# Cross-attention kernel: turned probabilities moved by DMA to one partition per key, value products in one matmul per head

## The chip, the cores and the metric

One Trainium2 chip (trn2), one NeuronCore of it. The metric is the device time of one execution in microseconds (us); lower is better. A core has TensorE (matmuls into PSUM), VectorE (DVE), ScalarE (ACT), GpSimd (POOL) and SyncE (SP), which here only issues DMAs. Each engine runs its own instruction stream in order, and they are tied together by semaphores.

## What is computed

`x` is 2 x 2048 x 640, the context 2 x 77 x 1024, with 69 text tokens and 8 image tokens (4 dummy, 4 of boxes). There are 20 heads of 32 columns.

```python
q = split(x @ w_q)
k, v = split(text @ w_k), split(text @ w_v)
out_text = softmax(q @ k.T / sqrt(32)) @ v
k_ip, v_ip = split(ip @ w_k_ip), split(ip @ w_v_ip)
out_ip = softmax(q @ k_ip.T / sqrt(32) + mask(bbox)) @ v_ip
out = (merge(out_text) + merge(out_ip)) @ w_out + b_out + x
```

The mask is 0 or -10000 by the position of the query in a 32 x 64 grid. All is float32.

## The kernel before

The work is 40 units. Unit c (`place(c)`) is one batch (2), one tile of 512 queries (4) and one group g of 128 model columns, which is 4 heads (5 groups). For a unit there are:

- `make_q`: the q product, transposed (128 columns x 512 queries), 15 matmuls of 128x128x512 in fp32r. Each operand is split into a high and a low part, so each of the 5 contraction blocks takes three matmuls (`product`, L604). It goes to PSUM bank 4; ScalarE copies it to `q`.
- `make_scores` (L637): 32 small fp32 matmuls, queries in the rows, 77 keys in the columns, into banks 0 to 3, a head per bank, columns 0 to 307. An fp32 matmul is two instructions, each with its own weight load.
- VectorE subtracts the text maximum, adds the mask and subtracts the image maximum (L466 to L483); ScalarE takes the exponential (L372); VectorE sums (`sums`, L490 to L495); GpSimd multiplies by the reciprocals (L334, L336). The result is `prob`: 128 queries in the partitions, 16 (query block, head) pairs x 96 columns, of which 77 are keys and the rest zero.
- `turn` (L502): VectorE transposes each 32x32 block. Afterwards a partition 32a + i holds key 32kb + i for the queries of the block a, so keys of all three key blocks kb lie on the same 32 partitions and queries are spread over four groups of partitions.
- `make_o` (L656): because of that the value products are 48 matmuls of 32x32 weights and 128 moving columns: 3 key blocks (accumulated) x 4 partition groups a x 4 heads. They write to columns 320 to 447 of banks 0 to 3, beside the scores. V lies four times, once on each 32 partitions, in three key blocks (`vt`, `v_turn` L728: 6 transposes per group; `v` is 128 x 6 x 640).
- `o_high` (ScalarE, L407) and `o_low` (VectorE, L508) split the result for the output product.
- `make_out`: 15 matmuls like those of q, into bank 5, six units behind; `finish` (VectorE, L519) adds bias and residual; SyncE stores the tile.

The order is written out by hand for every engine in `step(c)`. TensorE in a middle step: scores of c+1, q of c+2, value products of c-1, output product of c-6. Since scores and value products share banks, the scores of c wait for `o_low` of c-3 and the value products of c-1 wait until the scores of c+1 have been used. VectorE in a middle step: shifts of c+1, `turn(c)`, `o_low(c-1)`, `sums(c+1)`, `finish(c-6)`. ScalarE: `copy_q(c+2)`, `o_high(c-1)`, `exp(c+1)`, the high parts of newly loaded tiles. Steps 0 to 5 also hold the making of K and V for each group (context products L684, image products L690, whose output goes to a column group of 32 for each contraction block, turns L728), and the last two steps and the epilogue hold the output products without q.

SyncE issues all DMAs in order: prologue loads, in each step the loads of the step (`step_jobs`), then the residual of c-5 (waits until the tile's last store has landed) and the store of c-6 (waits for `finish`). Its queue also holds the V loads of groups 2 to 4 in the prologue, two of which wait for slots.

Of the kernel before, what the change touches and what calls it, by code (L numbers as in the profile page):

```python
# [41 lines left out]
V_OLD = {3: 0, 4: 2}  # L42
X_JOBS = {0: (0, 1, 2), 1: (3, 4)}
# [4 lines left out]
def xattn_kernel(nc, x, ctx, bbox, grid, eye, w_q, w_k, w_v, w_k_ip, w_v_ip, w_out, b_out, out):  # L48
# [22 lines left out]
    with es:  # L71
# [14 lines left out]
        eye_sb = sb("eye_sb", [P, P + BATCH * (KEYS - TEXT)])  # L86
        ident = eye_sb[:, 0:P]
        fold = eye_sb[:, P:P + BATCH * (KEYS - TEXT)].rearrange("p (b n) -> p b n", b=BATCH)
        vt = sb("vt", [P, BATCH * KB, QB, SQ])
# [25 lines left out]
        Q_BANK, OUT_BANK, SPARE_BANK = 4, 5, 6  # L115
        LAST_BANKS = [Q_BANK, SPARE_BANK, OUT_BANK, 0, 1]
        O_COL = 320
        o_blocks = ps[:, 0:QB, O_COL:O_COL + QT * SQ].rearrange("p a (n r) -> p n a r", r=SQ)
# [5 lines left out]
        v_place = ps[:, V_BANK, 0:BATCH * KEYS].rearrange("p (b n) -> p b n", b=BATCH)  # L124
        v_turned = ps[:, V_BANK:V_BANK + 2, :].rearrange("p b (k n) -> p (b k) n", n=P)[:, 2:2 + BATCH * KB, :]
# [37 lines left out]
        turned = sem("turned")  # L163
        o_made = sem("o_made")
# [27 lines left out]
        def is_late(c):  # L192
            return c >= UNITS - LATE

# [24 lines left out]
        def _(sp):  # L219
# [33 lines left out]
            def prologue():  # L253
# [21 lines left out]
                for job in step_jobs(0):  # L275
                    load(job)
                load_v(1, wv_raw, w_v, wv_loaded)
                load_v(1, wvi_raw, w_v_ip, wvi_loaded)
                load_k(4, wk_raw, w_k, wk_loaded)
                load_k(4, wki_raw, w_k_ip, wki_loaded)  # L280
                for job in step_jobs(1):
                    load(job)
                sp.dma_start(bias[:, :], b_out).then_inc(bias_loaded, 16)
                for g in range(2, KD):
                    load_v(g, wv_raw, w_v, wv_loaded)
                    load_v(g, wvi_raw, w_v_ip, wvi_loaded)

            def step(c):
                if c >= 2:
                    for job in step_jobs(c):  # L290
                        load(job)
# [56 lines left out]
        def _(act):  # L348
# [40 lines left out]
            def copy_vt(g):  # L389

                act.wait_ge(vt_made, g + 1)
                if g > 0:
                    act.wait_ge(v_made, g)
                nc.scalar.activation(vt[:, :, :, :], v_place.rearrange("p b (k r) -> p (b k) r", r=SQ)
                                     .unsqueeze(2).to_broadcast([P, BATCH * KB, QB, SQ]), ACT.Copy).then_inc(vt_copied, 1)

            def copy_v(g):

                act.wait_ge(v_made, g + 1)
                nc.scalar.activation(v[:, :, P * g:P * g + P], v_turned, ACT.Copy).then_inc(v_copied, 1)  # L400

            def o_high(c):
                b, t, g = place(c)
                act.wait_ge(o_made, c + 1)
                if c >= 2 * KD:
                    act.wait_ge(out_made, (c // KD - 1) * KD)
                nc.scalar.activation(o_hi[:, b, g, :].rearrange("p (n a r) -> p n a r", a=QB, r=SQ), o_blocks,  # L407
                                     ACT.Copy).then_inc(o_hi_done, 1)
# [18 lines left out]
            def step(c):  # L427
                if c <= KD:
                    if c + AHEAD_K < KD:
                        copy_k(c + AHEAD_K)  # L430
                    if c > 0:
                        copy_v_part(c - 1)
                        copy_vt(c - 1)
                    exp(c + AHEAD_S)
                    if c > 0:
                        copy_v(c - 1)
                    copy_q(c + AHEAD_Q)
                    if c > 0:
                        o_high(c - 1)
                    if c + AHEAD_K + 1 < KD:  # L440
                        copy_k_part(c + AHEAD_K + 1)
                elif exists(c + AHEAD_Q):
                    copy_q(c + AHEAD_Q)
                    o_high(c - 1)
                    exp(c + AHEAD_S)
                else:
                    if exists(c + AHEAD_S):
                        exp(c + AHEAD_S)
                    o_high(c - 1)
# [8 lines left out]
        def _(dve):  # L458
# [38 lines left out]
            def turn(c):  # L497

                dve.wait_ge(prob_done, c + 1)
                if c >= 2:  # L500
                    dve.wait_ge(o_made, c - 1)
                nc.vector.transpose(prob_t[:, c % 2, :, :].rearrange("p n k -> p (n k)"),  # L502
                                    prob[:, c % 2, :, :].rearrange("p n k -> p (n k)")).then_inc(turned, 1)

            def o_low(c):
                b, t, g = place(c)
                dve.wait_ge(o_hi_done, c + 1)
                nc.vector.tensor_tensor(o_lo[:, b, g, :].rearrange("p (n a r) -> p n a r", a=QB, r=SQ), o_blocks,  # L508
                                        o_hi[:, b, g, :].bitcast(F32).rearrange("p (n a r) -> p n a r", a=QB, r=SQ),
                                        ALU.subtract).then_inc(o_lo_done, 1)  # L510

            def finish(c, bank=OUT_BANK):
# [4 lines left out]
                if c == 0:  # L517
                    dve.wait_ge(bias_loaded, 16)
                nc.vector.scalar_tensor_tensor(out=tile, in0=ps[:, bank, :],  # L519
# [49 lines left out]
            def step(c):  # L569
                late = c >= UNITS - AHEAD_Q  # L570
# [3 lines left out]
                if late:  # L574
                    finish(c - BEHIND_OUT)
                if c == UNITS - 1:
                    o_low(c - 1)
                turn(c)
                if (late or c <= KD) and exists(c + AHEAD_S):
                    sums(c + AHEAD_S)  # L580
                if exists(c - 1) and c < UNITS - 1:
                    o_low(c - 1)
                if exists(c + AHEAD_S) and not late and c > KD:
                    sums(c + AHEAD_S)
# [266 lines left out]
```

## Time and profile before

| what | us |
|---|---|
| median of 3 runs | 438.83 |
| lowest and highest | 437.2, 440.38 |
| the profiled execution's own time | 438.98 |
| span of its trace | 437.2 |
| TensorE busy | 420.8 |
| VectorE busy | 346.8 |
| GpSimd busy | 155.3 |
| ScalarE busy | 134.0 |

The profile is of one execution. The span is the time from the first to the last instruction that the profiler saw. Busy time of TensorE counts overlapping matmuls once; the start of one block of matmuls to the start of the next says more of what a block costs than the sum of its durations. L604 is line 604 of the kernel. A wait is put down to what ended it.

### The profile page before, as it was taken

Reading aid. Unit: us, or ns where it says so; the run is one execution under the profiler, and the core shown is the slowest. Engines: PE = TensorE matmul, PEld = TensorE weight load, DVE = VectorE, ACT = ScalarE, POOL = GpSimd, SP = SyncE. Lnnn points to the kernel's source line nnn. Section 1 sums busy time; section 2 is a strip of 40 time slices with the busy share of each in tenths; the row PEclk is TensorE's granted clock in tenths of the full one; section 3 lists DMA queues with packets and bytes.
Section 4 is the critical chain, followed back from the end, with each engine's and each line's share of the span. In section 5 each row is a group of like instructions: output and inputs, shape, how many; then the busy total and the mean of one; then the engine's idle time right before and its main releaser. Section 6 shows DMA issues by size and latency. Waiting matters only on the chain.

```text
span 437.2 us, 17242 instructions
## 1 busy us (share of the span) xinstructions
PE 420.8 (96%) x7970; PEld 326.7 (75%) x7970; DVE 346.8 (79%) x457; ACT 134.0 (31%) x196; POOL 155.3 (36%) x128
## 2 busy tenths in 40 slices
PE   4999799989999999999999999999999999999996
PEld 3788678767777777777777777777777777777785
DVE  4578477759888998899888988899888988888712
ACT  4255344434223322342223332332223422222200
POOL 0238222555343632255324622265225422322200
PEclk9999999989999999999999999999999999999999
DMA  8987224212214321331124211321134111122333
GB/s 293 385 298 270 90 79 156 75 55 81 81 50 147 99 74 51 124 99 49 59 82 157 74 51 49 123 99 73 51 118 127 51 51 49 57 69 60 110 124 121
DMA packets 22391, 47.14 MB, mean 108 GB/s; under 512 B 2864, under 2 KB 2992, under 8 KB 22320
## 3 DMA queue, kind: packets, MB, share of 16 engines
q1 hardware_dynamic: 22320, 46.05, 30.7%
q8 instruction: 62, 1.02, 1.0%
q14 instruction: 9, 0.07, 0.1%
HBM read 35.55 MB, written 10.49 MB: 105 GB/s over the span
## 4 chain that ended last, share of the span: by engine, by line
PE 95%; DVE 2%; issue 1%; DMA 1%; ACT 0%
PE ps L604 67%; PE ps L656 13%; PE ps L637 8%; PE ps L684 5%; PE ps L690 1%; DMA stage<-in_w_q 1%; PE ps L728 1%; DVE prob_t L502 0%; PE ps L708 0%; DVE text_max L466 0%; DVE prob L472 0%; DVE wq_lo L558 0%; DVE stage L519 0%; ACT wq_hi L362 0%; PE ps L723 0%
## 5 line engine op out<-in xcount | busy, mean ns | idle before, releaser
L334 POOL TENSOR_TENSOR prob<-prob,rden 128x1104 f32<-128x1104 f32 x40 | 82.4, 2060 | 238.3 <-DVE rden L495 238.3
L604 PE MATMUL ps<-x_hi,wq_hi 128*128 128x512 f32 x200 | 84.9, 425 | 6.2 <-DVE x_lo L562 6.2
L368 ACT ACTIVATE q<-ps 128x512 f32<-128x512 f32 x40 | 23.8, 596 | 202.2 <-PE ps L604 202.2
L604 PE MATMUL ps<-o_hi,wo_hi 128*128 128x512 f32 x200 | 82.7, 414 | 0.0
L604 PE MATMUL ps<-x_lo,wq_hi 128*128 128x512 f32 x200 | 79.8, 399 | 0.0
L604 PE MATMUL ps<-x_hi,wq_lo 128*128 128x512 f32 x200 | 79.6, 398 | 0.0
L604 PE MATMUL ps<-o_lo,wo_hi 128*128 128x512 f32 x200 | 79.1, 395 | 0.0
L604 PE MATMUL ps<-o_hi,wo_lo 128*128 128x512 f32 x200 | 79.0, 395 | 0.0
L502 DVE STREAM_TRANSPOSE prob_t<-prob 128x1536 f32<-128x1536 f32 x40 | 70.8, 1769 | 0.0
L490 DVE TENSOR_REDUCE den<-prob 128x16 f32<-128x1104 f32 x40 | 51.9, 1296 | 19.0 <-ACT prob L372 19.0
L466 DVE TENSOR_REDUCE text_max<-ps 128x16 f32<-128x1104 f32 x40 | 52.2, 1304 | 17.3 <-PE ps L637 13.2
L656 PE MATMUL ps<-prob_t,v 32*32 32x128 f32 x3840 | 59.4, 278 | 1.7 <-DVE prob_t L502 1.7
L656 PEld LDWEIGHTS ps<-prob_t,v 32*32 32x32 f32 x3840 | 44.9, 103 | 19.9 <-issue 12.7
L372 ACT ACTIVATE prob<-prob 128x1232 f32<-128x1232 f32 x40 | 49.7, 1244 | 12.4 <-DVE prob L483 12.4
L472 DVE TENSOR_TENSOR prob<-ps,text_max 128x1104 f32<-128x1104 f32 x40 | 52.0, 1299 | 0.0
L604 PEld LDWEIGHTS ps<-x_hi,wq_hi 128*128 128x128 f32 x200 | 38.3, 191 | 17.2 <-DVE wq_lo L558 6.2
L604 PEld LDWEIGHTS ps<-o_hi,wo_hi 128*128 128x128 f32 x200 | 37.4, 187 | 14.6 <-issue 7.0
L508 DVE TENSOR_TENSOR o_lo<-ps,o_hi 128x512 fp32r<-128x512 f32 x40 | 27.1, 677 | 24.0 <-ACT o_hi L407 24.0
L637 PEld LDWEIGHTS ps<-k,q 32*64 32x64 f32 x2560 | 32.0, 130 | 18.2 <-issue 17.5
L318 POOL TENSOR_TENSOR x_lo<-stage,x_hi 128x512 fp32r<-128x512 f32 x35 | 44.4, 1293 | 1.7 <-ACT x_hi L359 1.7
L604 PEld LDWEIGHTS ps<-x_hi,wq_lo 128*128 128x128 f32 x200 | 38.1, 191 | 8.8
L604 PEld LDWEIGHTS ps<-o_hi,wo_lo 128*128 128x128 f32 x200 | 37.5, 187 | 9.1
(55 smaller groups left out, 387.0 us busy)
## 6 DMA issues: line engine op xcount, KB each, us to landing
stage<-in_x SPq DMA_DIRECT2D x38, 256.0 KB, 3.3
res<-in_x SPq DMA_DIRECT2D x37, 256.0 KB, 2.7
out_tiles<-res SPq DMA_DIRECT2D x37, 256.0 KB, 2.1
wk_raw<-in_w_k SPq DMA_DIRECT2D x5, 512.0 KB, 7.0
wki_raw<-in_w_k_ip SPq DMA_DIRECT2D x5, 512.0 KB, 6.4
wv_raw<-in_w_v SPq DMA_DIRECT2D x5, 512.0 KB, 6.2
wvi_raw<-in_w_v_ip SPq DMA_DIRECT2D x5, 512.0 KB, 7.7
stage<-in_w_q SPq DMA_DIRECT2D x5, 320.0 KB, 6.7
```

Of the source, the lines that this page charges most:

```text
L318: nc.gpsimd.tensor_tensor(x_lo[:, b, kt, :], slot[:, 0:W], x_hi[:, b, kt, :].bitcast(F32), ALU.subtract).then_inc(stage_lo, 1)
L334: nc.gpsimd.tensor_tensor(e[:, :, 0:TEXT], e[:, :, 0:TEXT], rden[:, par, 0, :].unsqueeze(2).to_broadcast([P, QT * HG, TEXT]), ALU.mult)
L368: nc.scalar.activation(q[:, c % 2, :], ps[:, Q_BANK, :], ACT.Copy, scale=SCALE).then_inc(q_copied, 1)
L372: nc.scalar.activation(prob[:, c % 2, :, 0:TOKENS], prob[:, c % 2, :, 0:TOKENS], ACT.Exp).then_inc(exp_done, 1)
L466: nc.vector.tensor_reduce(text_max[:, par, :, :], s[:, :, :, 0:TEXT], AX_X, ALU.max).then_inc(text_max_done, 1)
L472: nc.vector.tensor_tensor(e[:, :, :, 0:TEXT], s[:, :, :, 0:TEXT], text_max[:, par, :, :].unsqueeze(3).to_broadcast([P, QT, HG, TEXT]), ALU ...
L490: nc.vector.tensor_reduce(den[:, par, 0, :], e[:, :, 0:TEXT], AX_X, ALU.add)
L502: nc.vector.transpose(prob_t[:, c % 2, :, :].rearrange("p n k -> p (n k)"), prob[:, c % 2, :, :].rearrange("p n k -> p (n k)")).then_inc(t ...
L508: nc.vector.tensor_tensor(o_lo[:, b, g, :].rearrange("p (n a r) -> p n a r", a=QB, r=SQ), o_blocks, o_hi[:, b, g, :].bitcast(F32).rearrang ...
L604: return nc.tensor.matmul(ps[:, bank, :], w[:, g, P * kt:P * kt + P], m[:, b, kt, :], start=(n == 0), stop=(n == 3 * KD - 1))
L637: last = nc.tensor.matmul(ps[at:at + P // 2, j, TOKENS * n:TOKENS * n + TOKENS], q[rows, c % 2, P * n + at:P * n + at + P // 2], k[rows, b ...
L656: last = nc.tensor.matmul(ps[DH * j:DH * j + DH, a, O_COL:O_COL + QT * SQ], v[rows, KB * b + kb, P * g + DH * j:P * g + DH * j + DH], p_t[ ...
```

## The change

Of each unit's turned probabilities 12 DMAs on SyncE's queue copy the blocks from `prob_t` to a new tile `prob_k`, in which key k lies on partition k, for all 512 queries. `turn` writes the key block outermost, so that a DMA's rows are 2 KB. The value products become one matmul per head: 77 partitions, 32 columns of weights, 512 moving columns, into bank 7 alone. They run two units behind instead of one, right behind the scores; q and output products follow. `o_high` and `o_low` go two units behind too and read one plain bank. V is kept once, 77 partitions for each batch, so it takes two transposes per group instead of six, and smaller copies. The waits between scores and value products for their shared banks go. SyncE's V loads move: groups 1 and 2 before the last K load in step 0, groups 3 and 4 in steps 1 and 3. In the tail the output product of unit 33 goes to the q bank, the last tile's products use banks 6, 0, 1, 2, 3, and the value products of the last unit stand among them.

```diff
-        v = sb("v", [P, BATCH * KB, D])
+        v = sb("v", [P, BATCH, D])
...
-        prob_t = sb("prob_t", [P, 2, QT * HG, KEYS])
+        prob_t = sb("prob_t", [P, 2, KB, QT * HG, SQ])
+        prob_k = sb("prob_k", [P, 2, QB, QT * HG, SQ])
...
-        vt = sb("vt", [P, BATCH * KB, QB, SQ])
+        vt = sb("vt", [P, BATCH, TOKENS])
...
-        Q_BANK, OUT_BANK, SPARE_BANK = 4, 5, 6
-        LAST_BANKS = [Q_BANK, SPARE_BANK, OUT_BANK, 0, 1]
+        Q_BANK, OUT_BANK, O_BANK = 4, 5, 7
+        LAST_BANKS = [6, 0, 1, 2, 3]
...
+        def moves(c):
+
+            return 16 * QB * KB * (c // 2 + 1)
...
+            def move(c):
+
+                sp.wait_ge(turned, c + 1)
+                if c >= 2:
+                    sp.wait_ge(o_made, c - 1)
+                for kb in range(KB):
+                    n = min(SQ, TOKENS - SQ * kb)
+                    for a in range(QB):
+                        sp.dma_start(prob_k[SQ * kb:SQ * kb + n, c % 2, a, :, :],
+                                     prob_t[SQ * a:SQ * a + n, c % 2, kb, :, :]).then_inc(moved[c % 2], 16)
...
+            def step(c):
+                for job in step_jobs(c):
                     load(job)
...
+                if c == 0:
+                    for g in range(1, 3):
+                        load_v(g, wv_raw, w_v, wv_loaded)
+                        load_v(g, wvi_raw, w_v_ip, wvi_loaded)
+                    load_k(4, wk_raw, w_k, wk_loaded)
+                    load_k(4, wki_raw, w_k_ip, wki_loaded)
+                if c in V_OLD_STEP:
+                    load_v(V_OLD_STEP[c], wv_raw, w_v, wv_loaded)
+                    load_v(V_OLD_STEP[c], wvi_raw, w_v_ip, wvi_loaded)
+                move(c)
                 if exists(c - BEHIND_OUT + 1):
                     residual(c - BEHIND_OUT + 1)
...
                 if c >= 2:
-                    dve.wait_ge(o_made, c - 1)
-                nc.vector.transpose(prob_t[:, c % 2, :, :].rearrange("p n k -> p (n k)"),
-                                    prob[:, c % 2, :, :].rearrange("p n k -> p (n k)")).then_inc(turned, 1)
+                    dve.wait_ge(moved[c % 2], moves(c - 2))
+                nc.vector.transpose(prob_t[:, c % 2, :, :, :].rearrange("p k n r -> p n k r"),
+                                    prob[:, c % 2, :, :].rearrange("p n (k r) -> p n k r", r=SQ)).then_inc(turned, 1)
...
                 if c < KD:
                     pe.wait_ge(k_copied, c + 1)
-                if c >= 3:
-                    pe.wait_ge(o_lo_done, c - 2)
...
-                pe.wait_ge(turned, c + 1)
+                pe.wait_ge(moved[c % 2], moves(c))
                 if c < KD:
                     pe.wait_ge(v_copied, c + 1)
-                if exists(c + 2):
-                    pe.wait_ge(scores_used, c + 3)
                 if c >= 1:
                     pe.wait_ge(o_lo_done, c)
-                for kb in range(KB):
-                    for a in range(QB):
...
+                p_k = prob_k[0:TOKENS, c % 2, :, :, :].rearrange("p a (n h) r -> p n a h r", h=HG)
+                for j in range(HG):
+                    last = nc.tensor.matmul(ps[DH * j:DH * j + DH, O_BANK, :],
+                                            v[0:TOKENS, b, P * g + DH * j:P * g + DH * j + DH], p_k[:, :, :, j, :],
+                                            start=True, stop=True)
...
                     make_scores(c + AHEAD_S)
+                    make_o(c - 2)
                     make_q(c + AHEAD_Q, whole)
-                    make_o(c - 1)
-                    if exists(c - BEHIND_OUT):
-                        make_out(c - BEHIND_OUT)
+                    make_out(c - BEHIND_OUT)
...
             def epilogue():
...
+                make_out(UNITS - BEHIND_OUT)
+                make_o(UNITS - 2)
+                pe.wait_ge(scores_used, UNITS)
+                for g in range(3):
+                    make_last(g, range(0, KD - 2))
+                make_o(UNITS - 1)
+                for g in range(3):
+                    make_last(g, range(KD - 2, KD - 1))
                 for g in range(3):
                     make_last(g, range(KD - 1, KD))
```

VectorE's step becomes shifts of c+1, `o_low(c-2)`, `turn(c)`, `sums(c+1)`, `finish(c-6)`; ScalarE's middle step `o_high(c-2)`, `exp(c+1)`, `copy_q(c+2)`.

## Rows read from the trace of the kernel before

**Rows 1.** Page, parts 1 and 4: busy time by engine; the chain by line.

```profile
PE 420.8 (96%) x7970; PEld 326.7 (75%) x7970; DVE 346.8 (79%) x457; ACT 134.0 (31%) x196; POOL 155.3 (36%) x128
...
PE ps L604 67%; PE ps L656 13%; PE ps L637 8%; PE ps L684 5%; PE ps L690 1%; DMA stage<-in_w_q 1%; PE ps L728 1%; DVE prob_t L502 0%; PE ps L708 0%; DVE text_max L466 0%; DVE prob L472 0%; DVE wq_lo L558 0%; DVE stage L519 0%; ACT wq_hi L362 0%; PE ps L723 0%
```

**Rows 2.** Chain by time (start us, us, what): middle step, last piece.

```profile
217.59 3.65 PE ps L604 x15
221.23 1.42 PE ps L656 x79
222.65 3.70 PE ps L604 x15
226.34 0.88 PE ps L637 x57
...
416.22 17.70 PE ps L604 x75
```

**Rows 3.** VectorE's timeline, a middle step (start us, us, what, idle before).

```profile
227.26 1.31 DVE L466 TENSOR_REDUCE text_max<-ps 128x16 f32<-128x1104 f32 x1
...
230.55 1.77 DVE L502 STREAM_TRANSPOSE prob_t<-prob 128x1536 f32<-128x1536 f32 x1
232.95 0.69 DVE L508 TENSOR_TENSOR o_lo<-ps,o_hi 128x512 fp32r<-128x512 f32 x1 [0.63 <-ACT o_hi L407]
234.09 1.30 DVE L490 TENSOR_REDUCE den<-prob 128x16 f32<-128x1104 f32 x1 [0.45 <-ACT prob L372]
...
236.90 1.31 DVE L466 TENSOR_REDUCE text_max<-ps 128x16 f32<-128x1104 f32 x1
```

**Rows 4.** SyncE's queue: what it waited for (us in total, times, longest us).

```profile
SPq L251 <- DVE res L519: 237.7, 37, 9.0
```

**Rows 5.** Chain by time, early: image products, context products, turns of V.

```profile
19.62 0.57 PE ps L690 x16
...
22.47 1.88 PE ps L684 x16
...
38.65 0.66 PE ps L728 x6
```

**Rows 6.** Groups by line and form (xcount | busy us, mean ns | idle before).

```profile
L656 PE MATMUL ps<-prob_t,v 32*32 32x128 f32 x3840 | 59.4, 278 | 1.7 <-DVE prob_t L502 1.7
...
L690 PE MATMUL ps<-wki_raw,ctx_sb 128*32 128x128 f32 x80 | 3.2, 279 | 0.0
```

**Rows 7.** Waits of all engines (us in total, times, longest us).

```profile
PE ps L656 <- DVE prob_t L502: 1.7, 3, 1.0
```

**Rows 8.** Chain by time: the stall in step 2, step 5's end.

```profile
45.48 2.20 issue
...
85.36 1.47 PE ps L656 x75
...
87.76 0.61 ACT q L368
...
89.67 0.94 PE ps L637 x50
90.61 5.23 PE ps L604 x15
```

**Rows 9.** Windows: busy us by engine, then granted clock, DMA share, GB/s.

```profile
92.00:94.00 2.00, 2.00 (x6) 1.58 (x5) 1.93 (x5) 0.00 (x0) 1.19 (x1) 0.50 0.53 181
```

**Rows 10.** SyncE's timeline: DMA issues, at the start and in a middle step.

```profile
4.48 0.67 SPq L259 DMA_DIRECT2D grid_sb<-in_grid  x1
...
227.55 1.40 SPq L227 DMA_DIRECT2D stage<-in_x  x3
229.23 0.33 SPq L247 DMA_DIRECT2D res<-in_x  x1
```

**Rows 11.** Page, parts 3 and 6: packets, MB, share; us to landing.

```profile
q1 hardware_dynamic: 22320, 46.05, 30.7%
...
out_tiles<-res SPq DMA_DIRECT2D x37, 256.0 KB, 2.1
```

More of the change, by code:

```diff
@@ L42 @@
 V_OLD = {3: 0, 4: 2}
+V_OLD_STEP = {V_OLD[g] + 1: g for g in V_OLD}
 X_JOBS = {0: (0, 1, 2), 1: (3, 4)}
@@ L163, in xattn_kernel @@
         turned = sem("turned")
+        moved = [sem(f"moved{k}") for k in range(2)]
         o_made = sem("o_made")
@@ L274, in prologue @@
                 load_k(3, wki_raw, w_k_ip, wki_loaded)
-                for job in step_jobs(0):
+                sp.dma_start(bias[:, :], b_out).then_inc(bias_loaded, 16)
+            def step(c):
+                for job in step_jobs(c):
                     load(job)
[L277 to L291, printed above, removed]
+                if c == 0:
[8 more added lines that the diff above has]
+                move(c)
                 if exists(c - BEHIND_OUT + 1):
@@ L573, in step @@
                     shift_img(c + AHEAD_S)
-                if late:
+                if exists(c - 2):
+                    o_low(c - 2)
+                if c == UNITS - 1:
                     finish(c - BEHIND_OUT)
-                if c == UNITS - 1:
-                    o_low(c - 1)
                 turn(c)
-                if (late or c <= KD) and exists(c + AHEAD_S):
+                if exists(c + AHEAD_S):
                     sums(c + AHEAD_S)
[L581 to L584, printed above, removed]
-                if exists(c - BEHIND_OUT) and not late:
+                if exists(c - BEHIND_OUT) and c < UNITS - 1:
                     finish(c - BEHIND_OUT)
@@ L589, in epilogue @@
                 finish(UNITS - BEHIND_OUT)
-                o_low(UNITS - 1)
+                for c in range(UNITS - 2, UNITS):
+                    o_low(c)
                 for c in range(UNITS - KD, UNITS):
@@ L666, in make_out @@
                     pe.wait_ge(stage_lo, NUMBER[("w_out", g)] + 1)
-                if c >= 1:
-                    pe.wait_ge(finished, c)
+                if out_bank(c) == Q_BANK:
+                    pe.wait_ge(q_copied, UNITS)
+                elif c >= 1:
+                    pe.wait_ge(finished, c if out_bank(c - 1) == OUT_BANK else c - 1)
                 for n in whole:
-                    last = product(OUT_BANK, wo_hi, wo_lo, o_hi, o_lo, b, g, n)
+                    last = product(out_bank(c), wo_hi, wo_lo, o_hi, o_lo, b, g, n)
                 last.then_inc(out_made, 1)
@@ L722, in v_fold @@
                 pe.wait_ge(v_part_copied, g + 1)
-                nc.tensor.matmul(v_place[:, :, TEXT:KEYS], img_part[:, 1, :], fold, start=True, stop=True).then_inc(vt_made, 1)
+                nc.tensor.matmul(v_place[:, :, TEXT:TOKENS], img_part[:, 1, :], fold, start=True, stop=True).then_inc(vt_made, 1)
             def v_turn(g):
                 pe.wait_ge(vt_copied, g + 1)
-                for n in range(BATCH * KB):
-                    last = nc.tensor.transpose(v_turned[:, n, :], vt[:, n, :, :].rearrange("p a r -> p (a r)"), ident)
+                for b in range(BATCH):
+                    last = nc.tensor.transpose(v_turned[:, b, :], vt[:, b, :], ident)
                 last.then_inc(v_made, 1)
@@ L760, in early_step @@
                     v_turn(c - 1)
[L761 to L767 removed]
+                    make_q(c + AHEAD_Q, whole[9:15])
                 if c < 2:
```

75 lines of the change are left out of this document (27 added, 48 removed).

## The prediction

> **What bounds the kernel now.** I read the page first, then the chain of waits in order of time, then each engine's timeline over one middle step, SyncE's waits last. TensorE is busy for 420.8 us of 437.2, and the chain that ends last is TensorE almost all through: 67% products (L604), 13% value products (L656), 8% scores (L637) [rows 1]. In the chain a middle step is four blocks without idle time between them: q product 3.65, value products 1.42, output product 3.70, scores 0.88, in all 9.65 us [rows 2]. So a microsecond taken off TensorE in a middle step comes off the span, until another engine needs the whole step. VectorE is the nearest: from one text_max to the next 9.64 us, of which it idles 0.63 and 0.45 [rows 3], so its work is 8.56 us. That is the floor of a step as long as VectorE's work stays what it is. SyncE does nothing for most of the time: it waits 237.7 us in all for the finished tile [rows 4].
>
> **The change part by part.** All sums are made against the profiled execution: 438.98 us, 1.8 of it outside the span of 437.2. The median of the runs shown is 438.83, so the forecast for one is that for the other.
>
> *Value products.* Removed: 3840/40 = 96 TensorE instructions per unit on 32x32 tiles, 1.42 us from the block's start to the next. Added: 4 fp32 matmuls per unit (one per head, 77 partitions in, 32 columns of weights, 512 columns moving), each of two instructions, as all fp32 matmuls are here (48 matmuls give 96 instructions now). The trace has no such matmul, but it has its parts. An fp32 instruction that moves 138 columns takes 1.88/16 = 0.118 us, one of 128 columns 0.66/6 = 0.11 us, so 0.85 ns a column [rows 5]. Whether four heads run side by side is the main question. The image products (L690) are of the same form: all rows, 32 columns of weights, the four column groups in turn, another moving operand for each. 16 instructions of 128 columns take 0.57 us [rows 5, 6]; one after the other they would take 16 x 0.11 = 1.7. So four run together: 4 waves of 0.11 and some 0.13 for start and end. With 512 columns: 2 waves of 4 x 0.11 = 0.87, and 0.13, so 1.00 us. Bounds: 0.87 (no overhead) to 8 x 0.43 = 3.5 us (heads one after the other). I take 1.00, since L690 is the same shape but for its length. Gain: 0.42 x 40 = 16.8 us. The Trainium skill is a little more careful: "TensorE: Matmul & The Clock Gate", Part 3 (Packing small matmuls), gives 2.38 times the speed, not 3, for three column tiles of 32 with 512 columns; for four heads in the same proportion I estimate 3.2 times, so 4 x 0.87/3.2 = 1.1 us and a sum of 413. In the trace L690 comes to 1.7/0.57 = 3.0 times with its start and end in it.
>
> *Order on TensorE.* The value products move behind the scores, so q and output products stand next to each other. A block of 15 takes 3.70 and one of 75 takes 17.70 [rows 2]: 14.0/60 = 0.233 each, and 0.20 per block for changing over. One change-over less per step: 0.20 x 32 steps (6 to 37) = 6.4 us. Bounds 0, if what stands at a block's start is the wait and not the change of form, and 0.27 a step (3.65 + 3.70 - 30 x 17.70/75).
>
> *V plain.* Of 6 turns of V per early step, 2 remain: 4 x 0.11 x 5 = 2.2 us less [rows 5]. ScalarE's copies of it get smaller, which lies beside TensorE.
>
> *Early waits.* Now make_o(c-1) waits in the step in which its turn is made: 1.7 us on that tile's turn [rows 7], which in step 5 holds the products back until 85.36 [rows 8]. With a step more in between this goes. At the end of step 5 the scores wait for o_low in their own banks: TensorE ends the product at 87.76, where the copy of q begins, and starts again at 89.67, 1.91 us on [rows 8]. Value products have their own bank now, so only the copy of q (0.61, some 0.7 with its start) is left: gain 1.2. Behind this gap the clock is granted at 0.50 (1.2 GHz) for 92 to 94 [rows 9], and the q product takes 5.23 instead of 3.65: 1.6 us that I count as gained, since there is hardly a gap before it. The stall of 2.20 us inside the scores at 45.48 is put down to "issue" [rows 8]; nothing in the diff addresses it, but fewer instructions and another order of loads stand there; I count 1.1 of 0 to 2.2. New order of the early loads (V groups 1 and 2 before the last K): all have over 10 us until they are read; but I set 0.5 against it for a wait not foreseen.
>
> *The moves.* 12 DMAs per unit, 77 x 4 = 308 rows of 2 KB, 480 DMAs in all, on SyncE's queue between the loads and residual and store. Issue: 1.40/3 = 0.47 us each in a series, 0.67 for the worst kind in the trace [rows 10]; 0.33 is what a single one takes. I take 0.47, as all large ones in a series take this: 5.6 us per unit. Landing 2.1 as for the stores [rows 11]. In a step: scores end at 0.9, turn runs 4.8 to 6.6, moves are issued until 12.2 and have landed by about 14.3 from the step's start. They are needed two steps on, at 2 x 9.0 + 0.9 = 18.9, which leaves 4.6 us. SyncE per step: 5.6 + 2 x 0.33 for residual and store + at most 1.4 for loads = 7.7 of 9.0 us. Queued behind the wait for the turn are residual and store: the residual lands around 15, its finish comes at 18; the store is issued some 3 us later than now and its tile is needed again later still. Transfer: 22320 packets take 30.7% of 16 engines, 96 ns each [rows 11]; 308 x 96/16 = 1.9 us per unit, 17% of the engines' time over the span, beside 31% now. So all of it is hidden. In the tail it is less so: turn(38) ends 6.6 us into step 38, moves land at 14.3, TensorE is ready for O(38) at about 13.8: 0.5 us lost. O(39) stands behind 27 products (6.4 us), which cover its moves by about 1 us.
>
> *VectorE.* The turn writes the same 48 blocks to another place, 1.77 us as now [rows 3] (bounds 1.7 to twice that); o_low reads one bank plainly, 0.69 or a little less. The work stays 8.56 us.
>
> *Sum.* A middle step becomes 9.65 - 0.42 - 0.20 = 9.03 us, above VectorE's 8.56. In all 16.8 + 6.4 + 2.2 + 1.7 + 1.2 + 1.6 + 1.1 - 0.5 - 0.5 = 30.0, so 438.98 - 30.0 = 409.0 us.
>
> **The rivals.**
> *SyncE's queue becomes the bound; slower.* The step would be 12 issues and about 1.3 us for the rest. Above 0.64 us an issue this exceeds 9.03; from about 0.71 on the step is longer than now, as the value products then wait for the moves in each step. For it: 12 small DMAs a unit, a third of them of 13 partitions, a shape that the trace lacks, and 0.67 us for the smallest loads. Against: these lie in a full queue at the start and consist of short rows; the moves have 2 KB rows. At 0.80 us: 9.6 + 1.3 = 10.9 a step, 1.25 more than now in 34 steps, less 9 us of early gains: about 472 us. The Trainium skill, "DMA: Bandwidth & Descriptors", Rules for kernel authors, speaks for this rival: it tells to coalesce many small transfers, since below 64 KB one pays mostly overhead; the moves are of 64 and 26 KB. The trace agrees only in that a small load takes no less time to issue than a large one.
> *VectorE becomes the bound.* If the turn is slower with its split destination by over 0.47 us, the step is VectorE's. At twice its time: 8.56 + 1.77 = 10.33 a step, 0.7 more than now: 438.98 + 34 x 0.7 - 9 = 454. For it: 89% of the step is VectorE's already. Against: same number of blocks and bytes.
> *Heads one after the other.* 3.5 us a unit instead of 1.0: 409 + 100 = 509. Only the length differs from L690, so this is unlikely.
> *Half the side gains fail.* The step's order gives nothing, the clock falls in another place, the stall at 45 stays: 16.8 + 2.2 remain, 438.98 - 19 = 420. For it: TensorE gaps early moved before, and loads share the DMAs with moves there.
>
> **How the numbers follow.** Forecast (403 to 415) 0.68, side gains fail (415 to 425) 0.18, SyncE 0.06, VectorE 0.05, one after the other 0.03. The range from 402 to 425 holds the first two and leaves out the rest. A measurement here tells about 1% from no change: faster by over 1% 0.86, within 1% 0.04 (where SyncE or VectorE take back just the gain), slower 0.10.
>
> **What would show it.** Right: the value products are 320 instructions in blocks of about 1.0 us behind the scores; 30 products in one piece of about 7.15 us; middle steps of 9.0 us; no idle TensorE before the value products in steps 3 to 37; moves of 0.47 us, the last landing 4 us or more before its use; the turn at 1.77 us. Wrong: value products waiting for DMA prob_k in each step (SyncE), scores waiting for VectorE (VectorE), blocks of 3.5 us (no concurrency), 0.9 to 1.6 us more somewhere in the first 90 us (side gains).

## The result and the profile after

| | before | changed |
|---|---|---|
| median | 439.61 us (4 runs) | 483.72 us (4 runs) |
| lowest to highest | 437.2 to 441.04 | 478.04 to 485.29 |
| ratio, 95% interval | | 1.0943 (1.0885 to 1.1001) |

The changed kernel is slower by 9.4%, where 409.0 (402 to 425) was forecast. The profiled execution took 485.29 us, with a span of 483.5. The medians hold all executions, while each ratio leaves out those that stood apart from the rest of their kernel, here the one of 485.29 us, the profiled one, 0.3% above the median.

From the page of the changed kernel (span, part 1, the clock of part 2, part 3, both lines of part 4, three groups of part 5):

```profile
span 483.5 us, 10674 instructions
...
PE 419.3 (87%) x4430; PEld 303.4 (63%) x4430; DVE 335.5 (69%) x457; ACT 130.6 (27%) x196; POOL 155.9 (32%) x128
...
PEclk9999898898997999999899999899998999898959
...
q1 hardware_dynamic: 41840, 71.29, 51.2%
...
SPq 74%; PE 9%; issue 6%; DMA 5%; DVE 4%; ACT 1%; DVEq 0%
SPq L256 64%; PE ps L617 6%; SPq L267 3%; SPq L236 3%; SPq L271 3%; PE ps L692 1%; DMA stage<-in_x 1%; DVE prob_t L518 1%; DMA res<-in_x 1%; DMA prob_k<-prob_t 1%; DMA x_raw<-in_x 1%; PE ps L662 1%; DVE text_max L482 1%; DVE prob L488 1%; PE ps L698 0%
...
L536 DVE SCALAR_TENSOR_TENSOR res<-ps,bias,res 128x512 f32<-128x512 f32 x37 | 27.7, 751 | 93.6 <-DMA res<-in_x 79.3
...
L662 PE MATMUL ps<-prob_k,v 77*32 77x512 f32 x320 | 45.2, 638 | 30.9 <-DMA prob_k<-prob_t 21.4
L518 DVE STREAM_TRANSPOSE prob_t<-prob 128x1536 f32<-128x1536 f32 x40 | 70.7, 1767 | 0.0
```

The chain has changed hands. Before, it was TensorE for all but 5% [rows 1 give its lines: 67, 13 and 8%]; now 74% of it is SyncE's queue, and 64% of the span is one line of it, L256, the issue of the moves. TensorE is busy for about as long as before (419.3 for 420.8 us) in spite of 3540 fewer matmul instructions; the granted clock, which the page shows below 9 tenths in many slices, is 0.94 in the mean, 0.995 before. The run with four moves, further down, has the same 4430 instructions, a clock of 1.0 in the mean, and is busy for 392.7 us. VectorE waits before finish (L536) for 93.6 us, of which the residual's DMA ends 79.3. The turn takes 1767 ns, as before [rows 3], and it holds nothing up. The DMA engines' share is 51.2%, 30.7% before [rows 11].

A middle step in SyncE's queue, from the chain of the changed kernel in order of time (start us, us, what):

```profile
227.74 0.52 SPq L267
...
228.31 0.42 SPq L271
...
228.83 0.57 SPq L256
...
230.72 0.59 SPq L256
...
231.35 1.80 SPq L256
...
233.20 0.59 SPq L256
...
235.10 0.82 SPq L256
...
237.60 0.74 SPq L256
238.38 0.52 SPq L267
...
238.96 0.42 SPq L271
...
239.80 0.57 SPq L256
```

There is no gap: residual (L267), store (L271), twelve moves (L256), residual, store, and the moves of the next unit. From residual to residual it is 238.38 - 227.74 = 10.64 us; the queue never waits for anything in it. A move of 32 partitions takes 0.59 us and 0.04 to the next, one of 13 partitions 0.82, 0.78, 0.75, 0.74. One move of these takes 1.80. Before, a large issue took 0.47 in a series [rows 10], and SyncE spent 237.7 us waiting for finished tiles [rows 4]. What is left of its waits now (us in total, times, longest; L241 is a load of K at the start):

```profile
SPq L241 <- PE ps L716: 14.2, 2, 7.3
SPq L256 <- DVE prob_t L518: 8.8, 3, 4.5
...
SPq L267 <- DMA out_tiles<-res: 5.7, 2, 2.9
SPq L271 <- DVE res L536: 2.6, 2, 2.2
```

Who waits for SyncE instead, from all engines' waits:

```profile
DVE res L536 <- DMA res<-in_x: 79.3, 30, 11.6
...
PE ps L662 <- DMA prob_k<-prob_t: 21.4, 21, 3.6
...
PE ps L662 <- DVE o_lo L524: 9.4, 1, 9.4
```

Where the time went by part: the scores of unit 7 begin at 89.39 and those of unit 39 at 429.29 (TensorE's timeline).

```profile
89.39 0.82 PE L648 MATMUL ps<-k,q 32*64 32x77 f32 x52 [0.69 <-ACT q L386]
...
429.29 0.92 PE L648 MATMUL ps<-k,q 32*64 32x77 f32 x62
```

So the 32 middle steps take (429.29 - 89.39)/32 = 10.62 us each, 9.65 before [rows 2], 9.03 in the forecast. Single ones are not alike: ten of them are of 9.00 to 9.03 us, and those in which TensorE waits have up to 16.9 us. From there to the end of the span it is 54.2 us.

### The profile page after: what moved, and what is told of

It is laid out like the page before. It is cut to its first block, busy times and chain, and to the rows that moved or that the text cites. A ratio compares the mean times of both kernels' runs of the same rounds, so it can differ in the third digit from the quotient of the medians.

```text
span 483.5 us, 10674 instructions
## 1 busy us (share of the span) xinstructions
PE 419.3 (87%) x4430; PEld 303.4 (63%) x4430; DVE 335.5 (69%) x457; ACT 130.6 (27%) x196; POOL 155.9 (32%) x128
## 2 busy tenths in 40 slices
DMA packets 41888, 71.97 MB, mean 149 GB/s; under 512 B 10064, under 2 KB 10192, under 8 KB 41840
## 3 DMA queue, kind: packets, MB, share of 16 engines
q1 hardware_dynamic: 41840, 71.29, 51.2%
## 4 chain that ended last, share of the span: by engine, by line
SPq 74%; PE 9%; issue 6%; DMA 5%; DVE 4%; ACT 1%; DVEq 0%
SPq L256 64%; PE ps L617 6%; SPq L267 3%; SPq L236 3%; SPq L271 3%; PE ps L692 1%; DMA stage<-in_x 1%; DVE prob_t L518 1%; DMA res<-in_x 1%; DMA prob_k<-prob_t 1%; DMA x_raw<-in_x 1%; PE ps L662 1%; DVE text_max L482 1%; DVE prob L488 1%; PE ps L698 0%
## 5 line engine op out<-in xcount | busy, mean ns | idle before, releaser
L617 PE MATMUL ps<-o_hi,wo_hi 128*128 128x512 f32 x200 | 85.5, 428 | 18.2 <-DVE o_lo L524 17.7
L536 DVE SCALAR_TENSOR_TENSOR res<-ps,bias,res 128x512 f32<-128x512 f32 x37 | 27.7, 751 | 93.6 <-DMA res<-in_x 79.3
L617 PE MATMUL ps<-o_lo,wo_hi 128*128 128x512 f32 x200 | 83.4, 417 | 0.0
L617 PE MATMUL ps<-o_hi,wo_lo 128*128 128x512 f32 x200 | 82.9, 415 | 0.0
L662 PE MATMUL ps<-prob_k,v 77*32 77x512 f32 x320 | 45.2, 638 | 30.9 <-DMA prob_k<-prob_t 21.4
L518 DVE STREAM_TRANSPOSE prob_t<-prob 128x1536 f32<-128x1536 f32 x40 | 70.7, 1767 | 0.0
L617 PEld LDWEIGHTS ps<-o_hi,wo_hi 128*128 128x128 f32 x200 | 40.5, 203 | 35.2 <-DVE o_lo L524 20.5
L506 DVE TENSOR_REDUCE den<-prob 128x16 f32<-128x1104 f32 x40 | 50.6, 1265 | 9.1 <-ACT prob L390 9.0
L424 ACT ACTIVATE o_hi<-ps 128x512 fp32r<-128x512 f32 x40 | 23.6, 591 | 105.3 <-PE ps L662 105.3
L617 PEld LDWEIGHTS ps<-o_hi,wo_lo 128*128 128x128 f32 x200 | 40.3, 201 | 10.2
L617 PEld LDWEIGHTS ps<-o_lo,wo_hi 128*128 128x128 f32 x200 | 40.6, 203 | 9.3
L377 ACT ACTIVATE x_hi<-stage 128x512 fp32r<-128x512 f32 x35 | 21.8, 630 | 82.3 <-DMA stage<-in_x 82.0
```

Of the source, the lines that this page charges most:

```text
L424: nc.scalar.activation(o_hi[:, b, g, :], ps[:, O_BANK, :], ACT.Copy).then_inc(o_hi_done, 1)
L506: nc.vector.tensor_reduce(den[:, par, 0, :], e[:, :, 0:TEXT], AX_X, ALU.add)
L518: nc.vector.transpose(prob_t[:, c % 2, :, :, :].rearrange("p k n r -> p n k r"), prob[:, c % 2, :, :].rearrange("p n (k r) -> p n k r", r= ...
L617: return nc.tensor.matmul(ps[:, bank, :], w[:, g, P * kt:P * kt + P], m[:, b, kt, :], start=(n == 0), stop=(n == 3 * KD - 1))
L662: last = nc.tensor.matmul(ps[DH * j:DH * j + DH, O_BANK, :], v[0:TOKENS, b, P * g + DH * j:P * g + DH * j + DH], p_k[:, :, :, j, :], start ...
```

## The experiments

Theory A: SyncE's queue is the bound by its number of issues, at 0.63 to 0.86 us each. Theory B: the moves' transfer or landing is the bound. Theory C: the order is, since the residual now stands behind the moves. All ratios are to the kernel before in the same session (medians 440.17, 441.0 and 440.46 us). Differences from the changed kernel's 483.72 us are taken across sessions, between which the kernel before moved by 0.3% (439.61 to 441.0 us).

**Third key block as 16 partitions.**

```diff
-                    n = min(SQ, TOKENS - SQ * kb)
+                    n = min(SQ, TOKENS + 3 - SQ * kb)
```

> The third key block is moved as 16 partitions (keys 64 to 79, three of them zero columns) instead of 13; all else stays. Theory A (SyncE's issue of the moves is the bound; a 13-partition move takes 0.75 to 0.82 us to issue, a 32-partition one 0.59, because of its odd number of partitions): each of the 4 falls to about 0.59, 0.75 us less per unit, 27 to 30 us less in all, about 454 us. Theory B (the transfer or the landing of the moves is the bound): 3/77 more rows, so 483 or a little more. Theory C (the residual stands behind the moves and comes too late for finish): as A in proportion to the issue, a fall of at most 0.7 us a step.

Measured: 457.96 us, ratio 1.0403 (1.0335 to 1.0472). 26 us less than the changed kernel (483.72), though each of the 160 moves of the third block carries three rows more. The group of all 480 moves (duration ns min/median/max):

```profile
L256 SPq DMA_DIRECT2D prob_k<-prob_t x480: 507/590/2161, 32.6 to 434.9; - x160
```

The four issues of 0.74 to 0.82 us in the chain above are 0.59 us here, as A has it; the fall of 26 us is just short of the 27 to 30 expected. B is out for this part: more rows were moved, not fewer. C expected a fall of this size too, so the run says nothing against C.

**Four of the twelve issued by ScalarE.**

```diff
-                for kb in range(KB):
+                for kb in range(KB - 1):
...
+            def move_last(c):
+                act.wait_ge(turned, c + 1)
+                if c >= 2:
+                    act.wait_ge(o_made, c - 1)
+                kb = KB - 1
+                n = TOKENS - SQ * kb
+                for a in range(QB):
+                    act.dma_start(prob_k[SQ * kb:SQ * kb + n, c % 2, a, :, :],
+                                  prob_t[SQ * a:SQ * a + n, c % 2, kb, :, :]).then_inc(moved[c % 2], 16)
```

> The four 13-partition moves of each unit are issued by ScalarE, behind its copy of q; the eight others stay on SyncE. The same bytes are moved. Theory A: SyncE needs 8 x 0.63 + 1.05 for residual and store + about 0.6 for loads = 6.7 us a step, below TensorE's 9.0, so it is no longer the bound: 408 to 425 us. Theory B: the DMA engines move the same rows, so 475 to 490. Theory C: the residual comes 3.2 us earlier, so most of the gain too.

Measured: 424.64 us, ratio 0.9638 (0.9611 to 0.9665). The same rows and bytes, through the same 16 DMA engines, in as many DMAs that have to land, and 59 us less than the changed kernel: what bound it was SyncE's queue, not the transfer or the landing. C, by which the earlier residual gives most of the gain, is not out yet. Its waits, first in SyncE's queue, then all engines' (here ScalarE's):

```profile
SPq L256 <- DVE prob_t L530: 58.2, 37, 6.1
```

```profile
ACT x_hi L377 <- issue: 45.6, 12, 4.6
```

SyncE has time again (58.2 us waiting for the turn). ScalarE pays: 45.6 us in which its copies of x stand behind its own issues, and some products wait for that.

**Four moves a unit instead of twelve.** Only the first key block is moved.

```diff
-                for kb in range(KB):
+                for kb in range(1):
...
-            return 16 * QB * KB * (c // 2 + 1)
+            return 16 * QB * (c // 2 + 1)
```

> Left out: only the first key block is moved (4 DMAs a unit instead of 12); the other partitions of the moved tile are set to zero once. Theory A: SyncE is idle for most of the step and the rest of the forecast is laid open: middle steps of 9.0 us and 405 to 415 us in all. Theory B expects the same here. If the other terms of the forecast (value products 1.0 us, one change-over less, early waits) are wrong as well, it stays above 420.

Measured: 407.68 us, ratio 0.9256 (0.9232 to 0.9279). This is the forecast without the term that was wrong. A and B expect the same here, so the run does not tell them apart; it shows the other terms. A step in the chain of this run (start us, us, what):

```profile
206.09 0.99 PE ps L663 x8
207.08 7.13 PE ps L618 x30
214.21 0.88 PE ps L649 x56
215.09 0.99 PE ps L663 x8
```

Value products 0.99 (forecast 1.00, 1.42 before [rows 2]), q and output products in one piece of 30 in 7.13 (7.35 in two pieces before), scores 0.88: 9.00 us a step, where 9.03 was worked out. SyncE waits for the turn, longest in this list:

```profile
SPq L256 <- DVE prob_t L519: 165.1, 40, 6.1
```

The scores of units 7 and 39 begin here at

```profile
78.12 0.95 PE L649 MATMUL ps<-k,q 32*64 32x77 f32 x64 [0.69 <-ACT q L387]
...
367.42 0.80 PE L649 MATMUL ps<-k,q 32*64 32x77 f32 x50
```

which is 9.04 us a step. Against this run the changed kernel loses 89.39 - 78.12 = 11.3 us up to unit 7, 339.9 - 289.3 = 50.6 in the middle and 54.2 - 38.0 = 16.2 from unit 39 on: 78.1, the whole difference of the spans (483.5 - 405.4).

**The residual ahead of the moves.**

```diff
-                move(c)
                 if exists(c - BEHIND_OUT + 1):
                     residual(c - BEHIND_OUT + 1)
+                move(c)
```

> The residual is issued ahead of the moves in each step; the number of issues is the same. Theory A (rate of the queue): within 1.5% of the changed kernel, 476 to 490 us, and finish no longer waits for the residual, but the value products wait for the moves instead. Theory C (order): the wait of finish for the residual, 79 us in all, goes and with it most of the loss: below 455 us.

Measured: 511.55 us, ratio 1.1533 (1.1445 to 1.162). Neither theory expected 28 us more than the changed kernel. Its chain in order of time and, below it, SyncE's waits say why:

```profile
237.53 2.19 DMA out_tiles<-res
...
239.74 0.34 SPq L267
```

```profile
SPq L267 <- DMA out_tiles<-res: 48.7, 35, 2.4
```

From all engines' waits of this run:

```profile
PE ps L662 <- DMA prob_k<-prob_t: 57.9, 32, 4.3
...
DVE res L536 <- DMA res<-in_x: 5.8, 1, 5.8
```

The residual needs the tile whose store has just been issued. Behind the moves that store has long landed; ahead of them SyncE stands idle for its landing, 48.7 us in all in 35 waits or 1.4 us each. From unit 7 to unit 39 the first moves of two units are 11.50 us apart in the mean, in the changed kernel 10.67: (11.50 - 10.67) x 32 = 26.6 us, nearly the difference of the spans (510.5 - 483.5 = 27.0). Of the 48.7 us 5.7 were there before. Of the 43.0 that are new, 11 are got back in shorter issues (all of SyncE's sum to 400 us instead of 411), and its other waits change by less than 2 us each; the few us that are left were not traced. C is refuted: its own wait is gone (finish waits 5.8 us for the residual instead of 79.3), and the loss is not. What grew is the wait of the value products for the moves, 57.9 for 21.4, as A has it. A's size failed all the same, since it did not foresee the new wait: this queue has next to no time to spare, so most of a new wait in it comes out at the end.

**Half the bytes.** Each move takes half of each row.

```diff
-                        sp.dma_start(prob_k[SQ * kb:SQ * kb + n, c % 2, a, :, :],
-                                     prob_t[SQ * a:SQ * a + n, c % 2, kb, :, :]).then_inc(moved[c % 2], 16)
+                        sp.dma_start(prob_k[SQ * kb:SQ * kb + n, c % 2, a, 0:8, :],
+                                     prob_t[SQ * a:SQ * a + n, c % 2, kb, 0:8, :]).then_inc(moved[c % 2], 16)
```

> Left out: each of the 12 moves takes only the first half of each row (1 KB of 2 KB); the other half of the moved tile is set to zero once. Number of issues and of rows stay, the bytes are halved. Theory A (cost per issue): 0.59 and 0.78 us an issue as before, within 1.5% of the changed kernel, 476 to 490 us. Theory B (bytes, transfer): the issues get shorter and 20 us or more are won, below 465.

Measured: 475.65 us, ratio 1.0799 (1.0765 to 1.0834). This is 1.7% below the changed kernel's median, just outside what A expected; B's 20 us are not there. Twelve issues in this run (SyncE's timeline), 8.25 us, which is 8 x 0.63 and 4 x 0.80:

```profile
232.72 8.25 SPq L256 DMA_DIRECT2D prob_k<-prob_t  x12
```

The time of an issue does not hang on its bytes: for each of the twelve places in a unit the median over all units is that of the changed kernel to 0.001 us. The moves sum to 328 us for 336, and the difference lies in moves of over 0.9 us, 22 here and 27 there; why there are fewer was not tested.

**By way of DRAM, 4 DMAs a unit.** One DMA writes the turned tile out, three read it back with the keys in order.

```diff
+                sp.dma_start(via[c % 2], prob_t[:, c % 2, :, :, :].rearrange("p k n r -> p k (n r)")).then_inc(written[c % 2], 16)
...
+                for kb in range(KB):
+                    n = min(SQ, TOKENS + 3 - SQ * kb)
+                    sp.dma_start(prob_k[SQ * kb:SQ * kb + n, c % 2, :, :, :].rearrange("p a n r -> p a (n r)"),
+                                 via[c % 2].rearrange("(a i) k x -> i a k x", i=SQ)[0:n, :, kb, :]).then_inc(moved[c % 2], 16)
```

> The same result with 4 DMAs a unit instead of 12, all on SyncE: one writes the turned tile (128 partitions, 6 KB rows) to DRAM, and behind the store three read it back, one per key block (32, 32 and 16 partitions, 4 rows of 2 KB each). Theory A: at 0.45 to 0.60 us an issue 2.1 us of moves a step, SyncE is off the bound, and the time is that of the run with 4 moves, 407 to 414 us, as long as both trips (2.5 to 3.5 us each) fit into the 12 us between turn and use. Theory B: twice the DMA traffic of the changed kernel's moves, so no better than 475. If the round trip is too long for the tail: 3 to 6 us above 410.

Measured: 424.35 us, ratio 0.9636 (0.9597 to 0.9676), above the 407 to 414 of A. SyncE's timeline of a step, and below it all engines' waits (here TensorE's):

```profile
220.03 1.30 SPq L263 DMA_DIRECT2D prob_k<-via  x3
...
225.16 0.33 SPq L254 DMA_DIRECT2D via<-prob_t  x1
```

```profile
PE ps L670 <- DMA prob_k<-via: 12.2, 5, 5.5
```

The issues are cheap, 1.30 us for three and 0.33 for one, and 30 of the 32 middle steps take 8.99 to 9.02 us. What is lost is lost in a few places: 12.2 us of waiting in 5 times, the longest 5.5 us in step 2 (behind the scores of unit 3), where the first unit's write and reads stand behind the big loads of K and V. The theory's size for the landing, 2.5 to 3.5 us, was too low: in the middle the write lands after 3.9 us in the median and the reads after 4.2 and 4.6, and early the write takes 7.5. In the middle the two trips still fit between turn and use.

**ScalarE with 16 partitions.**

```diff
-                n = TOKENS - SQ * kb
+                n = TOKENS + 3 - SQ * kb
```

> As the run with ScalarE issuing the third key block, but with 16 partitions instead of 13. ScalarE's four issues take 0.6 instead of 0.8 us, 2.4 instead of 3.3 us a step, and its copies of x behind them and of the next value products come 0.8 us earlier. Theory: if ScalarE's blocked time is what holds the run with 13 at 424.6 above 407.7, half to all of it goes: 409 to 417 us. If it is the DMA traffic, it stays at 423 to 427.

Measured: 422.85 us, ratio 0.9584 (0.9535 to 0.9633): 1.8 us less than with 13 partitions, at the edge of what the runs tell apart. The edit took little of ScalarE's blocked time away (its copies of x stand 35.7 us behind its own issues instead of 45.6), so this run alone does not clear it. The last run below does: there it is 40.6 us, at a time of 412.08. The trace puts a loss elsewhere: 6.5 us in one piece before the value products of unit 39. It is there in the changed kernel too, where it is 9.45 us:

```profile
452.75 8.26 SPq L256 DMA_DIRECT2D prob_k<-prob_t  x12
461.06 0.52 SPq L267 DMA_DIRECT2D res<-in_x  x1
...
464.34 0.75 DVE L536 SCALAR_TENSOR_TENSOR res<-ps,bias,res 128x512 f32<-128x512 f32 x1 [11.62 <-DMA res<-in_x]
465.01 0.68 DVE L524 TENSOR_TENSOR o_lo<-ps,o_hi 128x512 fp32r<-128x512 f32 x1
...
465.83 1.94 PE L662 MATMUL ps<-prob_k,v 77*32 77x512 f32 x8 [9.45 <-DVE o_lo L524]
```

(Changed kernel, the timelines of SyncE, VectorE and TensorE.) The twelve moves of unit 39 stand ahead of the residual of unit 34; finish(34) waits for that residual, `o_low(38)` stands behind it on VectorE, and the last value products need `o_low(38)`. TensorE starts them at 465.83, 9.45 us late. The forecast priced the moves of the tail, but not what is queued behind them.

**Both repairs.** Units 0 to 4, 38 and 39 move directly, with 4 (at the end 6) of 12 issues on ScalarE; units 5 to 37 go through DRAM; the loads of V groups 1 and 2 stand behind the first moves; in the last two steps the residual stands ahead.

```diff
+        def direct(c):
+            return c < KD or c >= UNITS - 2
...
+                if c >= UNITS - 2:
+                    residual(c - BEHIND_OUT + 1)
+                if direct(c):
+                    move_part(sp, c, split(c)[0])
+                else:
+                    write(c)
+                if c == 0:
+                    for g in range(1, 3):
+                        load_v(g, wv_raw, w_v, wv_loaded)
+                        load_v(g, wvi_raw, w_v_ip, wvi_loaded)
```

> A kernel that is to keep the gains, with the reference's output. Units 0 to 4 and 38, 39: direct moves (third key block as 16 partitions), part of them issued by ScalarE (4 of 12, at the end 6 of 12); units 5 to 37: the way through DRAM, 4 DMAs. In step 0 the loads of V groups 1 and 2 stand behind the moves, in the last two steps the residual stands ahead of them. Theory (what is left above the run with 4 moves is early moves behind big loads and the late residual at the end): middle steps 9.0, step 3 under 12, step 39 to the end about 39, so 408 to 414 us. If DMA traffic in the early part is at fault: 416 to 422.

Measured: 413.0 us, ratio 0.9401 (0.9351 to 0.945), as expected. The middle steps are of 9.06 us, step 3 of 10.8 (under 12 expected), and from the scores of unit 39 to the end it is 40.6 us, where about 39 was expected.

**Three DMAs of 128 partitions.** A measurement of the issue itself; keys are not rearranged.

```diff
+                for kb in range(KB):
+                    sp.dma_start(prob_k[:, c % 2, kb, :, :], prob_t[:, c % 2, kb, :, :]).then_inc(moved[c % 2], 16)
```

> Left out: the rearranging. Each unit moves its turned tile by 3 DMAs of 128 partitions (64 KB becomes 256 KB each), partition to same partition, so keys are not in order. It measures what one DMA from SBUF to SBUF costs in issue. If 0.59 us is the price of both ends in SBUF: 0.59 here too. If it is the price of few partitions: 0.43 to 0.47, as the loads of 128 partitions. Either way 1.3 to 1.8 us a unit, and the time is that of the run with 4 moves, 405 to 412, though more bytes are moved than in the changed kernel (786 KB for 631).

Measured: 405.79 us, ratio 0.9231 (0.9168 to 0.9293). SyncE's timeline, three issues together:

```profile
221.09 1.76 SPq L254 DMA_DIRECT2D prob_k<-prob_t  x3
```

The first takes 0.47 us, the two others 0.60 and 0.62. So 0.6 us is the price in a series of a DMA with both ends in SBUF, of 32 partitions or of 128; the loads from DRAM that follow one another take 0.43 to 0.47 in the same queue. The residual, also a load from DRAM, takes 0.60 here, where it stands directly behind the third move, and 0.33 to 0.34 where the queue was idle before it (the kernel before [rows 10] and the run with the residual ahead). So the price may in part be that of standing behind a move; the runs do not tell the two apart. And 786 KB a unit in three DMAs cost nothing that can be seen, where 631 KB in twelve cost 78 us: the bytes are out. With the run of four issues on ScalarE, in which all twelve still have to land, B is out altogether.

**Direct moves, split over two queues, with the repairs.** As the kernel with both repairs, with no unit by way of DRAM: 8 issues on SyncE and 4 on ScalarE a unit, 6 and 6 for the last two.

```diff
-            return c < KD or c >= UNITS - 2
+            return c < UNITS or c >= UNITS - 2
```

> As the kernel before in this list (early order, residual ahead at the end), but all units move directly, 8 issues by SyncE and 4 by ScalarE, 6 and 6 for the last two units. Theory: the same early part and end; the middle steps cost what they do in the run with 16 partitions on ScalarE (9.0 to 9.2), so 2 to 5 us more than the kernel by way of DRAM: 411 to 418.

Measured: 412.08 us, ratio 0.9374 (0.9308 to 0.944). One of the four executions took 634.95 us at a mean granted clock of 0.563, where the three others took 408.87 to 412.71 at 0.995 or more; no cause was found for it. From the page of the one of 408.87 us (span, busy time, granted clock in 40 slices):

```profile
span 407.1 us, 10712 instructions
...
PE 394.5 (97%) x4430; PEld 289.2 (71%) x4430; DVE 335.1 (82%) x457; ACT 129.7 (32%) x196; POOL 155.6 (38%) x128
...
PEclk9999999999999999999999999999999999999999
```

It beats the kernel before by 6.3% (the kernel by way of DRAM has 6.0%; the intervals overlap, so which is better stays open) and the changed one by 14%. In the profiled execution the clock stays at 9 tenths or more in all 40 slices. What the two repairs give can be read by part: against the run with 16 partitions on ScalarE, from which it differs in them alone but for two issues in each of the last two units, the span is 4.9 us shorter up to the scores of unit 7, 1.5 in the 32 steps behind them, and 8.6 from unit 39 on.

## Why the prediction was wrong, point by point

**The step that failed** is the price of a move: "I take 0.47, as all large ones in a series take this: 5.6 us per unit." It measured 0.63 us from start to start for 32 partitions and 0.78 to 0.86 for 13, 8 x 0.63 + 4 x 0.81 = 8.3 us a unit, and in most units one issue is longer still (1.80 in the step shown), so the twelve take up to 9.9 us, 8.9 in the mean of the middle steps (0.74 each); from the first move of unit 7 to that of unit 39 a unit takes 10.67 us in the mean. The bound of 0.67 from the small loads stood in the text, and even without the long issues the mean of 0.69 (8.3/12) lies just above it. The sum took its price from loads out of DRAM that follow one another; the moves go from SBUF to SBUF, and the trace of the kernel before had no row of that kind.

**SyncE per step**, 7.7 of 9.0 us: it was 10.6 in the step shown. With it fell "So all of it is hidden".

**The rival that came true** is SyncE's queue, which had 0.06. The measured price is on its side of its point of decision (0.64 us an issue for being the bound), and its 472 us at 0.80 was nearer than the forecast. Its price for the rest of the queue, 1.3 us, was too low: residual, store, loads and short waits take 1.8 us in the mean of the middle steps. That shows in the run with 16 partitions: at 0.68 us an issue this rival's sum gives a step of 9.5 us, shorter than the 9.65 of before, and the step measured is 10.0. It left out that the tail loses in proportion: 16.2 us from unit 39 on, where I had 0.5 us.

**Heads side by side**: right. 0.99 us for 1.00. In the trace the first instructions of the four heads start within 0.02 us of each other, and the second ones 0.45 us later. One after the other the eight would take 3.4 us by the prediction's price, so four heads side by side are 3.5 times as fast. The estimate from the proportion in the Trainium skill ("TensorE: Matmul & The Clock Gate", Part 3) was 1.1 us, somewhat more than measured.

**One change-over less**: right. 7.35 became 7.13, 0.22 for 0.20.

**Early waits, clock and stall**: right in kind, as the run with four moves shows, and too low in size. It loses 0.69 us at the end of step 5 (0.7 forecast), the scores of unit 3 have no stall, and all 40 slices of its page have a granted clock of 9 tenths or more. Its 407.68 us answers to 409.0, in part by luck. Up to the scores of unit 7 it gains 11.6 us on the kernel before (89.67 [rows 8] to 78.12), of which one value product, 1.0 us, is only put off; the terms of the sum for this part come to 7.8 (2.2 + 1.7 + 1.2 + 1.1 - 0.5, and five value products of 0.42). The stall gave all of its 2.2 us where 1.1 was counted; the rest of the difference was not traced. But in the changed kernel itself these gains were not there: every wait for the moves is a gap, and behind some of these gaps the clock falls, as here. TensorE's timeline with the gap:

```profile
229.12 1.06 PE L662 MATMUL ps<-prob_k,v 77*32 77x512 f32 x8 [1.31 <-DMA prob_k<-prob_t]
```

A stretch some 2 us behind it (start and end us, length, PE, PEld, DVE, ACT, POOL busy, granted clock, DMA share, GB/s):

```profile
231.00:234.50 3.50, 3.50 (x10) 2.73 (x9) 3.47 (x5) 0.00 (x0) 0.18 (x1) 0.51 0.37 95
```

A granted clock of 0.51 is the level of 1.2 GHz. At 233 us a product of this stretch takes 0.43 us from start to start, 0.23 elsewhere.

**Transfer**: too low, without consequence. The queue's packets grew by 41840 - 22320 = 19520 [rows 11], or 488 a unit where 308 was assumed, and their time by 51.2% of 483.5 us less 30.7% of 437.2, which is 2.8 us a unit where 1.9 was forecast. By the runs with fewer bytes and with more, it was not the bound.

**VectorE**: right. The turn into split blocks takes 1.767 us, 1.769 before.

**Coalescing**: the Trainium skill ("DMA: Bandwidth & Descriptors", Rules for kernel authors) spoke against this change, and on the result it was right. Its reason, overhead per transfer, agrees with the runs: halving the bytes gave 1.7%, three DMAs for twelve gave 16%. The same page (Issuing engines are not separate DMA queues) says that issuing from more engines saves only issue time, usually small beside the transfer. Here that issue time was the bound, and spreading it gave 12% (424.64 for 483.72).

## What to carry to other kernels

Count the issues of an in-order DMA queue like instructions of an engine: number by price, with the price taken from a row of the same kind (both ends, number of partitions), and compare the sum with the step; a queue that mostly waits is free only until that sum passes the step. When the price is unknown within a factor that contains the point of decision (here 0.64 us between bounds of 0.33 and 0.67), the range must reach to the other side and the chance of it is not small. And where small DMAs can't be avoided, split them over two issuing engines, give them 16 or 32 partitions rather than 13, or go through DRAM with few large ones; and look at what stands behind them in the queue at the end of the kernel.

## What the runs showed of the hardware that was not expected

- A DMA of 13 partitions takes 0.74 to 0.82 us to issue, one of 16 or 32 partitions 0.59, one of 128 also 0.60, all from SBUF to SBUF in a series on SyncE. No other counts were measured, so what it is about 13 stays open. Loads from DRAM of 128 partitions take 0.43 to 0.47 behind one another, and 0.52 to 0.60 directly behind a move (the residual: 0.52 in the changed kernel, 0.60 in the run with three DMAs).
- Some issues take 1.0 to 2.1 us. In the changed kernel's trace there are 32 of over 0.9 us among SyncE's 635; 31 of them lie at the start of one of the 35 transfers of instructions in the trace, and in the run with four moves 10 of 10. This is a coincidence in time in two traces, not shown as a cause; no run took the transfers away.
- With two queues at once (the run with four of twelve on ScalarE) the issues get a little longer where they overlap: SyncE's fourth to sixth move of a unit takes 0.76 to 0.82 us beside ScalarE's of 13 partitions, 0.59 to 0.65 beside ScalarE's of 16, 0.59 alone (medians over 40 units).
